# Routing of a mixture of experts by pairs of tiles in split fp32r products, with the slot table laid out by position

## What is computed

```python
logits = x @ gate_weight.T;  scores = sigmoid(logits);  sfc = scores + e_bias          # 64 experts
group_scores = top_k(sfc.reshape(T, 8, 8), 2)[0].sum(-1);  gidx = top_k(group_scores, 4)
tmp = where(in a chosen group, sfc, 0);  topk_idx = top_k(tmp, 8)
topk_w = scores[topk_idx];  topk_w = 2.5 * topk_w / (topk_w.sum(-1) + 1e-20)
# per expert: up to 512 tokens, in order of their index; a token's position is its rank in the expert
h = silu(xe @ w1.T) * (xe @ w3.T);  ye = h @ w2.T;  out[token] += ye * topk_w
shared = (silu(x @ shared_gate.T) * (x @ shared_up.T)) @ shared_down.T                  # for all tokens
x = layernorm(x + out + shared)
```

## Time and profile before

| | us |
|---|---|
| median of 3 runs | 3635.91 (3630.8 to 3637.6) |
| profiled execution | 3647.32 |
| its span | 3645.4 |
| attention stages, to the start of routing | 2541 |
| routing and shared expert, to the last scatter | 2541 to 3054 |
| between the routing loop and the first full unit | 3054 to 3089 |
| experts | 3089 to 3600 |
| last norm | 3600 to 3645 |

### The profile page before, as it was taken

One profiled execution on the slowest core, in us unless ns is written; L12 is line 12 of the kernel. 1 busy time (PEld: TensorE's weight loads), 2 busy tenths in 40 slices (PEclk: granted clock), 3 DMA queues, 4 the chain that ended last, 5 costly groups with the idle time before them and its releaser, 6 DMA issues. The chain is left out here.

```text
span 3645.4 us, 63837 instructions
## 1 busy us (share of the span) xinstructions
PE 3178.9 (87%) x18593; PEld 2049.0 (56%) x18593; DVE 2199.4 (60%) x4889; ACT 1384.6 (38%) x3155; POOL 1557.1 (43%) x1113
## 2 busy tenths in 40 slices
PE   7998989999898998989796999997988883999991
PEld 4444444444445444454344777774767762888880
DVE  4645556564554645556253888885566663777775
ACT  1443434444353443435221666663000000454441
POOL 3342434424243342425431333342466564566661
PEclk8998999999999999999898999998999996999995
DMA  4122121222202122120372212212322112789986
GB/s 119 39 67 71 33 71 36 68 71 67 72 21 79 39 67 71 47 59 3 120 264 90 62 62 68 62 62 75 76 55 52 51 50 84 222 252 248 254 252 211
DMA packets 188692, 343.99 MB, mean 94 GB/s; under 512 B 36153, under 2 KB 53946, under 8 KB 187450
## 3 DMA queue, kind: packets, MB, share of 16 engines
q1 hardware_dynamic: 132282, 242.51, 23.8%
q0 software_dynamic: 28800, 48.43, 5.9%
q10 hardware_dynamic: 27392, 50.34, 3.7%
HBM read 206.96 MB, written 83.89 MB: 80 GB/s over the span
## 5 line engine op out<-in xcount | busy, mean ns | idle before, releaser
L544 ACT ACTIVATE sa_probs<-sa_s 128x512 f32<-128x512 f32 (+3 forms) x1280 | 614.9, 537 | 744.6 <-PE sa_s L435 413.1
L329 POOL TENSOR_TENSOR sa_both<-sa_probs 128x2048 f32<-128x2048 f32 (+2 forms) x160 | 589.9, 3687 | 692.2 <-PE sa_pv L462 680.7
L401 PE MATMUL sa_w<-sa_parts 96*128 96x512 f32 (+3 forms) x1280 | 518.4, 457 | 115.7 <-DVE sa_pmax L603 35.9
L435 PE MATMUL sa_s<-sa_parts 128*128 128x512 f32 (+3 forms) x1280 | 460.0, 410 | 18.9 <-ACT sa_probs L544 13.6
L607 DVE TENSOR_REDUCE sa_pmax<-sa_w 128x1 f32<-128x512 f32 (+3 forms) x768 | 419.1, 584 | 86.3 <-PE sa_w L401 83.0
L401 PEld LDWEIGHTS sa_w<-sa_parts 96*128 96x128 f32 x1280 | 237.9, 196 | 408.1 <-DVE sa_pmax L603 120.7
L603 DVE CUSTOM_DVE_ANT_0 sa_w<-sa_w,sa_maskS 128x512 f32<-128x512 f32 (+3 forms) x512 | 326.2, 649 | 229.9 <-PE sa_w L401 223.7
L1385 POOL DMA_INDIRECT token_and_weight_of_slot<-rt_entry,rt_sl x256 | 254.8, 995 | 151.2 <-DVE rt_entry L1554 75.9
L435 PEld LDWEIGHTS sa_s<-sa_parts 128*128 128x128 f32 x1280 | 244.3, 195 | 130.5 <-ACT sa_probs L544 64.4
L453 PE MATMUL sa_pv<-sa_probs,sa_values 128*32 128x512 f32 (+3 forms) x2560 | 274.7, 548 | 0.0
L1202 ACT ACTIVATE xa_sm<-xa_sm,xa_nmax 128x154 f32<-128x154 f32 x512 | 208.8, 410 | 64.4 <-DVE xa_nmax L1146 64.4
(11 more groups left out here) (243 smaller groups left out, 5821.9 us busy)
## 6 DMA issues: line engine op xcount, KB each, us to landing
ex_w<-in_w SPq DMA_DIRECT2D x138, 512.0 KB
sa_parts<-sa_halves SPq DMA_DIRECT2D x384, 128.0 KB, 2.4
sa_xt<-in_xT SPq DMA_DIRECT2D x32, 1024.0 KB
scratch_attention_T<-sa_oT SPq DMA_DIRECT2D x32, 256.0 KB, 2.2
on_at<-scratch_attention_T SPq DMA_DIRECT2D x32, 256.0 KB, 3.3
on_xr<-in_x SPq DMA_DIRECT2D x32, 256.0 KB, 3.4
scratch_x<-on_xn ACTq DMA_DIRECT2D x32, 256.0 KB, 2.1
scratch_x_T<-on_xnT ACTq DMA_DIRECT2D x32, 256.0 KB, 3.4
```

What stands on the lines that cost most here:

```text
L329: pool.tensor_tensor(both[:, :, 0:w], probs[:, even, :, 0:w], probs[:, odd, :, 0:w], ALU.add).then_inc(both_ready, 1)
L401: nc.tensor.matmul(ps[:, 0:w], qparts[0:3 * HD, h, q0:q0 + P], kparts[0:3 * HD, h, k0:k0 + w], start=True, stop=True).then_inc(work_ready, 1)
L435: mm = nc.tensor.matmul(ps[:, 0:w], kparts[:, h, kb * P:(kb + 1) * P], qparts[:, h, q0:q0 + w], start=True, stop=not diag)
L544: nc.scalar.activation(probs[:, r % NPB, h, 0:w], sbank[n % NSB][:, 0:w], ACT.Exp).then_inc(exp_done, 1)
```

## The change

The tiles of `route_and_shared` are taken in 16 pairs. The products of the shared expert no longer run in float32 but in three products of fp32r halves (`TERMS`), with 256 columns in the gate and up products; the halves of x, of the hidden layer and, once at the start, of the three weights are made by ScalarE (high) and VectorE (low). The scores stay in float32. `choose`, `locate` and the sigmoid of the scores serve both tiles at once. VectorE no longer picks the eight weights: it normalises the whole row of 64 (`wn`), and SP stores it behind the token's row in `x2`, whose rows grow from 512 to 576 floats (`ROW`). The table holds the token alone, 4 bytes a slot; a slot is position x 64 + expert. GpSimd loses `rt_oh`. TensorE's loop has one pair in its body, the other engines' loops two. `experts` reads the table by position and expert, so that it needs no turning, gathers rows of 2304 bytes and takes `factor` out of the gathered row. Cross-attention stores to `x2` with the new row length.

```diff
-LIM = 1.0e6
+ROW = DM + E_
...
+        def each_pair(eng, body):
+            each_tile(eng, body, NPR)
...
+                def load_x(p):
+                    wait(sp, gate_done, p)
+                    apart(sp, passed)
+                    wait(sp, xl_done, p * 2)
+                    apart(sp, passed)
+                    sp.dma_start(xT[:].rearrange("p n k t -> p n (k t)"),
+                                 x2T[bass.ds(p * 2, 2)].rearrange("n p k t -> p n (k t)")).then_inc(xT_in, 16)
...
+                def body(p, s):
+                    wait(sp, r_done, p * 2 - 2)
+                    sp.dma_start(xr[:, s], pair_rows(x2, p)[:, :, 0:DM]).then_inc(x_in[s], 16)
+                    if more(p, 2):
+                        load_x(p + 2)
+                    sp.wait_ge(wn_done, p + 1)
+                    sp.dma_start(pair_rows(x2, p)[:, :, DM:ROW], wn[:, s]).then_inc(wn_out[s], 16)
+                each_pair(sp, body)
                 sp.wait_ge(spare_set, 32)
...
-                    pool.wait_ge(eq_done, t + 1)
-                    wait(pool, w8_done, t)
-                    pool.tensor_tensor(oh[:], eq[:], wden[:, s].unsqueeze(1).broadcast_to([P, 8, E_]), ALU.mult).then_inc(oh_done, 1)
...
+                    if not isinstance(p, int) or p >= 2:
+                        pool.wait_ge(scat[s], ((p - s) // 2) * 256)
+                    pool.tensor_copy(entry[:, s], tokall[:, bass.ds(p * 2, 2)]).then_inc(tok_done, 1)
+                    pool.wait_ge(tok_done, p + 1)
+                    pool.wait_ge(slot_done, p + 1)
                     apart(pool, passed)
-                    for k in range(TOPK):
-
-                        pool.indirect_dma_start(out=table, out_offset=bass.IndirectOffsetOnAxis(ap=sl[:, s, k:k + 1], axis=0),
-                                                in_=entry[:, s, k], in_offset=None, bounds_check=SLOTS - 1,
-                                                oob_is_err=False).then_inc(scat[s], 16)
-                each_tile(pool, body)
+                    for j in range(2):
+                        for k in range(TOPK):
+
+                            pool.indirect_dma_start(out=table, out_offset=bass.IndirectOffsetOnAxis(ap=sl[:, s, j, k:k + 1], axis=0),
+                                                    in_=entry[:, s, j:j + 1], in_offset=None, bounds_check=SLOTS - 1,
+                                                    oob_is_err=False).then_inc(scat[s], 16)
+                each_pair(pool, body)
...
+                def up(p):
+                    pe.wait_ge(xl_done, p * 2 + 2)
+                    for half in range(2):
+                        wait(pe, hT_done, p * 2 + (half - 1))
+                        for n, (w, o, done) in enumerate(((wgh, gg[half], gg_done), (wuh, uu[half], uu_done))):
+                            if isinstance(p, int) and p == 0 and half == 0:
+                                pe.wait_ge(w_low, n + 1)
+                            for f in range(2):
+                                c = (2 * half + f) * P
+                                for k in range(KT):
+                                    for i, (a, b) in enumerate(TERMS):
+                                        mm = nc.tensor.matmul(o[:, f * W2:(f + 1) * W2], w[:, a, k, c:c + P], xh[:, b, k],
+                                                              start=k == 0 and i == 0, stop=k == KT - 1 and i == len(TERMS) - 1)
...
+                    pe.wait_ge(hl_done, p * 2 + 2)
+                    if isinstance(p, int) and p == 0:
+                        pe.wait_ge(w_low, 3)
+                    for j in range(2):
+                        wait(pe, r_done, p * 2 + (j - 1))
+                        for n, (a, b) in enumerate(TERMS):
+                            for f in range(KT):
+                                mm = nc.tensor.matmul(dd[j][:], hTh[:, a, f, j * P:(j + 1) * P], wdh[:, b, f],
+                                                      start=n == 0 and f == 0, stop=n == len(TERMS) - 1 and f == KT - 1)
...
+                def body(p):
+                    score(p + 1)
+                    rank(p)
+                    up(p + 1)
+                    down(p)
+
+                score(0)
+                up(0)
+                body(0)
+                with pe.Fori(1, NPR - 1) as p:
+                    body(p)
+                rank(NPR - 1)
+                down(NPR - 1)
...
+                def high_x(p):
+                    act.wait_ge(xT_in, p * 16 + 16)
+                    wait(act, uu_done, p * 2)
+                    for j in range(2):
+                        nc.scalar.copy(xh[:, 0, :, j * P:(j + 1) * P], xT[:, j]).then_inc(xh_done, 1)
...
+                def high_hidden(p, half):
+                    act.wait_ge(hT_done, p * 2 + (half + 1))
+                    wait(act, dn_done, p * 2)
+                    nc.scalar.copy(hTh[:, 0, 2 * half:2 * half + 2].rearrange("p f t -> p (f t)"), hT[:, half]).then_inc(hh_done, 1)
...
+                def body(p, s):
+                    if more(p, 1):
+                        gates(p + 1, 1 - s)
+                        for half in range(2):
+                            sigmoid(p + 1, half)
+                    if more(p, 2):
+                        high_x(p + 2)
+                    if more(p, 1):
+                        for half in range(2):
+                            high_hidden(p + 1, half)
+                    act.wait_ge(r_done, p * 2 + 2)
+                    act.dma_start(pair_rows(res, p), r[:, s]).then_inc(r_out[s], 16)
...
+                def low_x(p):
+                    for j in range(2):
+                        dve.wait_ge(xh_done, p * 2 + (j + 1))
+                        dve.tensor_tensor(xh[:, 1, :, j * P:(j + 1) * P], xT[:, j], xh[:, 0, :, j * P:(j + 1) * P],
+                                          ALU.subtract).then_inc(xl_done, 1)
...
+                    dve.wait_ge(pos_done, p + 1)
+                    dve.wait_ge(sel_done, p + 1)
+                    dve.tensor_tensor(cum[:], cum[:], sel[:, s, 0], ALU.add).then_inc(cum_done, 1)
+                    dve.tensor_tensor(kk[:, s], pps[:, 0:2 * E_].rearrange("p (n e) -> p n e", n=2),
+                                      eb1[:].unsqueeze(1).broadcast_to([P, 2, E_]), ALU.add).then_inc(kk_done, 1)
+                    dve.wait_ge(cum_done, p * 2 + 1)
+                    dve.tensor_tensor(cum[:], cum[:], sel[:, s, 1], ALU.add).then_inc(cum_done, 1)
+                    dve.wait_ge(kk_done, p * 2 + 1)
...
+                    if not isinstance(p, int) or p >= 2:
+                        dve.wait_ge(scat[s], ((p - s) // 2) * 256)
                     apart(dve, passed)
-                    step(dve.tensor_tensor(pi[:], pi[:], ki[:], ALU.add))
-
-                    if not isinstance(t, int) or t >= 2:
-                        dve.wait_ge(scat[s], ((t - s) // 2) * 128)
+                    dve.tensor_tensor(sl[:, s].rearrange("p n k -> p (n k)"), kf[:], ef[:], ALU.add).then_inc(slot_done, 1)
+                    dve.wait_ge(wsum_done, p + 1)
+                    step(dve.tensor_scalar(wrec[:], wsum[:, s], 1.0e-20, None, ALU.add))
+                    step(dve.reciprocal(wrec[:], wrec[:]))
+                    assert n == PLACES
+                    stored(dve, wn_out, p, s)
                     apart(dve, passed)
...
+                def finish(p, s):
+                    fetched(dve, x_in, p, s)
+                    stored(dve, r_out, p, s)
+                    for j in range(2):
+                        dve.wait_ge(dn_done, p * 2 + (j + 1))
+                        dve.tensor_tensor(r[:, s, j], dd[j][:], xr[:, s, j], ALU.add).then_inc(r_done, 1)
...
+                def body(p, s):
+                    if more(p, 1):
+                        choose(p + 1, 1 - s)
+                        hidden(p + 1, 0)
+                    locate(p, s)
+                    if more(p, 1):
+                        hidden(p + 1, 1)
+                    if more(p, 2):
+                        low_x(p + 2)
+                    finish(p, s)
+                    if more(p, 1):
+                        for half in range(2):
+                            low_hidden(p + 1, half)
+                each_pair(dve, body)
...
+            sp.dma_start(entries[:], table.rearrange("(n p e) c -> p n (e c)", p=P, e=E_)).then_inc(entries_in, 16)
...
-                pool.tensor_copy(factor[:, s], weight[:, bass.ds(unit * J, J)]).then_inc(factor_set, 1)
+                pool.wait_ge(xe_in[s], turn_of(w, s) * (16 * J))
+                apart(pool, passed)
+                pool.tensor_copy(factor[:, s], xe[:, s, :, bass.ds(unit // UPE + DM, 1)].rearrange("p j c -> p (j c)")).then_inc(factor_set, 1)
...
-            pe.wait_ge(entries_in, 16)
-            for c in range(2):
-                for a in range(HALVES):
-                    mm = nc.tensor.transpose(h1[0][:, (c * HALVES + a) * P:(c * HALVES + a + 1) * P], entries[:, a, :, c], identf[:])
-            mm.then_inc(entries_turned, 1)
-            pe.wait_ge(listed, 2)
...
```

(6 more changed lines are left out.)

366 lines of the change are left out of this document (164 added, 202 removed).

## The result

| | kernel before | changed kernel |
|---|---|---|
| median of the runs | 3631.89 us (3625.14 to 3637.6, 6 runs) | 3655.14 us (3645.01 to 3658.18, 6 runs) |
| profiled execution: time, span | 3647.32, 3645.4 | 3645.01, 3642.7 |
| ratio after to before | | 1.0052, 95% interval 1.0035 to 1.0069 |
| first scatter / start of the last | 2577.57 / 3053.00 | 2580.77 / 3050.51 |
| routing by tile or pair | 15.05 us a tile, 30.1 a pair | 30.04 us a pair |

The forecast was 3541 us, so it was wrong by 114 us, and in sign: the change made the kernel half a per cent slower. The loop's pace, which was to fall from 30.1 to 23.0 us a pair, did not move.

What follows compares the result with a forecast made beforehand. A chain through GpSimd's scatters and VectorE was taken to bound routing. Loop minus 104, experts' start minus 2.5 and wider rows plus 12 gave minus 94.5: 3552.8 profiled, 3541 us as median (3505 to 3600).

Steps and rivals of the forecast that it cites:

- first scatter: Start of routing: after splitting the weights and the first pair's chain, GpSimd's first scatter comes at 2584.5 us (2580 to 2590).
- a scatter, mean and gap: Routing loop, GpSimd: each scatter takes 0.996 us, up to 1.04 with VectorE's splits, with 0.30 us between scatters.
- GpSimd's round: Routing loop: 16 scatters, a copy and holding by VectorE's splits make 22.5 us a pair.
- TensorE's pair without holes: Routing loop: split products, scores and ranks of a pair take TensorE 18.8 us at full clock.
- TensorE's pair with holes: Routing loop: with the slower clock and unreleased idle gaps as frequent per scatter as before, TensorE takes 23.5 us a pair.
- loop, end of the last scatter: Routing loop at 23.0 us a pair: the last scatter ends at 2950.0 against 3054.0, minus 104 us.
- from there to the first gather: Start of the experts: no turning of the table and an earlier load save 2.5 us (0 to 5).
- from the first gather on (the wider rows): Experts: rows of 2304 instead of 2048 bytes cost 0.27 us in each of 45 units, plus 12 us (0 to 35).
- TensorE's share: Routing loop: products of 18.8 us a pair, some 20 at clock 0.92 to 0.96, 23.5 with holes per scatter as now.
- GpSimd held in long batches: Rival, routing loop: each eight scatters cost GpSimd 2.23 us more, 27.0 us a pair, 3606 us; chance 0.13.
- gathers that break up: Rival, experts: each gathered row becomes two pieces, costing 35 to 50 us, 3564 to 3579 us; chance 0.08.
- VectorE holding every scatter: Rival, routing loop: each scatter takes 1.62 us instead of 0.996, 31.8 us a pair, 3683 us; chance 0.05.

Runs made afterwards that it cites:

- b_same_c: The kernel before, unedited, run and traced on a chip without holes: 3610.0 us.
- a_few: The changed kernel with 2 of its 16 scatters a pair, on a chip where the kernel before took 3606.1 us: 3448.4 us.
- a_same_c: The changed kernel, unedited, on a chip without holes where the kernel before took 3605.7 us: 3529.5 us, ratio 0.9782.
- a_half_b: The changed kernel with only the first tile's eight scatters a pair, on a chip with holes (kernel before 3633.5 us): 3474.8 us.

## Why the prediction was wrong, point by point

| step | forecast | chips with holes | chips without |
|---|---|---|---|
| first scatter | 2584.5 (2580 to 2590) | 2580.8 | 2580.6 |
| a scatter, mean and gap | 0.996 to 1.04, 0.30 | 1.01, 0.30 | 1.02, 0.30 |
| GpSimd's round | 22.5 a pair | hidden | 22.2, sets the pace |
| TensorE's pair without holes | 18.8 | hidden | 18.76 |
| TensorE's pair with holes | 23.5 | 30.0, sets the pace | no holes |
| loop, end of the last scatter | 2950, minus 104 | 3051.5, minus 2.5 | 2933.7, minus 83.6 against b_same_c |
| from there to the first gather | minus 2.5 | minus 1.0 | minus 0.3 |
| from the first gather on (the wider rows) | plus 12 | plus 0.8 | plus 3.4 |
| time | 3541 (3505 to 3600) | 3655 | 3529.5 |

**The step that failed** is in the paragraph on TensorE's share: "If they come as often per scatter as now, a pair is 23.5." Holes do not come per scatter. Within one program they grow with the length of a run, and the change keeps the 256 scatters and doubles the runs. By runs the trace of before would have said so: its holes open about 9 us into a run of eight, which lasts 10, and close 1.5 us behind it (medians of its runs). Ten more microseconds of the same run had to be priced at that rate of loss, not at the mean over all scatters. In the run shown above, the stretch with holes lasts 10.3 us (2746.2 to 2756.5) and holds nine products, 1.1 us of work at full clock. With 9 us lost to it a pair is 18.8 plus 9, 28, and most of the gain is gone before the clock is counted. The second term missed is the clock. I let it slow 18.8 us to 20 (0.92 to 0.96); over 2590 to 2890 it was 0.80. It is granted in full or in half, and falls to half 14 times in the loop, each time within one of the 14 stretches of holes, in which TensorE idles. In the run shown (half from 2748.7 to 2762.4) this costs 2.2 us behind the holes (5.17 for 2.96), and 28 plus 2.2 is the 30 measured. The busy time of 22.9 holds both, since products that crawl through the holes count as busy.

**What VectorE and GpSimd did** followed from it. The scores of the next pair wait in TensorE's order, `choose` starts late and is itself drawn out, and the slots come 7 to 13 us after GpSimd has asked for them. VectorE's own load was no problem: in a_few it keeps up with 18.8 us a pair.

**The rivals.** The first, GpSimd held in long batches, had the right observation (holes fall where a run of eight ends, the cause not seen, two runs now back to back) and the wrong engine: I let GpSimd be held and gave it 2.23 us an eight. GpSimd's scatters keep their 1.28 us on every chip, with two gaps of 2.2 to 2.3 us in the whole loop, on chips of either kind (the trace of before has two as well, at 2790.73 and 3005.41, where I counted one); the others are held. Its size, 27.0 a pair, was also too small. The second, gathers that break up, did not happen: 5632 packets of 4096 bytes in the experts before, 5632 of 4608 after. The third, VectorE holding every scatter, did not either: the mean over all scatters is 1.01 us. On what the Trainium skill says (SBUF — State Buffer, section SBUF: two separate sides) of operations that exclude each other for a whole instruction, the trace agrees in kind: of the 26 scatters over 1.05 us, 25 have one of VectorE's splits beside them. But only 50 scatters meet a split, and their mean is 1.14 against 0.975 for the other 206, half a microsecond a pair (0.66 in a_same_c, where I had put 0.7), and that decided nothing.

**What was right.** On chips without holes the time is 3529.5, in the range and 12 us from the forecast; the pace there was made by the engine named, at the size named. That the time came so close is in part luck: the kernel before is 30 us faster there than the 3636 that I started from, and the gain is 76 us and not 94.5. I counted 12 us for wider gathered rows. From the first gather to the end it is 564.5 us before (3080.94 to 3645.4) and 565.3 after (3077.45 to 3642.7); b_same_c and a_same_c differ by 3.4 (564.0 and 567.4). So 65.5 KB more in a unit cost 0.02 to 0.07 us, not 0.27, little more than one kernel's traces differ among themselves (564.0 to 566.1 before). The lower bound, that the idle 0.14 of the DMA engines hides them, was the better value, and lower also than the 7 us by the fit of the Trainium skill (DMA: Bandwidth & Descriptors, section Anatomy of one DMA — SWDGE (gpsimd) path). Together with a loop that gains 83.6 and not 104, because the kernel before also runs faster there (27.7 us a pair and not 30.1), this gives the 0.978.

**What remains open.** What keeps the instructions away. The list of queues in the changed kernel for 2720 to 2980, in which holes fall in every pair, has data packets only:

```profile
q1 hardware_dynamic: 6800, 9.44, 12.0%
q10 hardware_dynamic: 2176, 4.19, 4.3%
q0 software_dynamic: 4192, 0.08, 1.2%
```

No queue for instructions appears there, so TensorE is not waiting for code that the trace shows being loaded. The list of the whole span has two:

```profile
q8 instruction: 110, 1.80, 0.2%
q14 instruction: 108, 0.88, 0.1%
```

The Trainium skill (Runtime: NRT & Kernel Launch, section Instruction fetch mechanics) describes each sequencer as fetching code through a DMA queue of its own in blocks. The trace shows blocks on two queues outside this stretch and none in it. Which engines those two serve it does not say, so a late block on a queue that is not recorded is not ruled out. The regular spacing fits some small portion that is delivered late, but that is an argument and not shown.

## What to carry to other kernels

Price a stall by where it stands, not by its mean: if it opens at the end of a run of like instructions, doubling the run at the same count makes it many times longer. Before scatters of several tiles are put together, look whether "issue" gaps on TensorE line up with the ends of runs of GpSimd's indirect transfers; where they do, don't lengthen the runs, and put several microseconds of other work between them. How short is short enough this case does not settle: runs of eight cost 9 us in all in a_half_b, and 52 to 57 in the kernel before. And a change whose gain hangs on such stalls has no single ratio: measure it on more than one chip before believing either sign.
